# Queries turned by VectorE and regrouped through DRAM, causal chunks of 32 queries, weighted sums directly ahead of scores

## What is computed

```
q = (x @ wq.T)  32 heads of 32;   k, v = x @ wk.T, x @ wv.T   8 heads of 32
q = q * cos + rotate_half(q) * sin          (k the same)
scores = q k^T / sqrt(32), causal;  attn = softmax(scores);  out = attn v
x = layernorm(x + out @ wo.T)
```

## Time and profile before

| | |
|---|---|
| median of 3 runs | 1434.85 us (1432.27 to 1437.24) |
| the profiled execution | 1439.9 us |
| its span, first to last instruction | 1438.1 us |
| busy share PE / DVE / ACT / POOL | 95% / 76% / 65% / 69% |
| DMA | 213.03 MB, mean 148 GB/s |
| last matmul of part 1 ends | about 784 us into the span |

### The profile page before, as it was taken

The page is one execution under the profiler, slowest core; times in us unless marked ns, Lnnn a source line. Parts: engine busy times, 40 slices in busy tenths (PEclk is TensorE's granted clock), DMA queues, the critical chain, the costliest instruction groups (busy, mean ns, idle before and its releaser), DMA issues. The chain is left out here.

```text
span 1438.1 us, 32297 instructions
## 1 busy us (share of the span) xinstructions
PE 1370.1 (95%) x8288; PEld 1061.4 (74%) x8288; DVE 1092.5 (76%) x3869; ACT 932.5 (65%) x3258; POOL 985.9 (69%) x936
## 2 busy tenths in 40 slices
PE   6899999999999999999985899999999999999995
PEld 4677777777777777777753688888888888888874
DVE  5677777777777777777766477878887788887784
ACT  5678878788787887878765354555554455555542
POOL 3677767777677776777754566777766777776753
PEclk9999999999999999999996899999999999999997
DMA  6345445454454544545465857656666766666751
GB/s 227 113 121 156 122 139 152 119 155 122 141 152 119 152 125 141 151 119 153 125 179 164 218 145 170 165 153 163 159 159 165 175 150 159 165 156 162 157 117 44
DMA packets 108861, 213.03 MB, mean 148 GB/s; under 512 B 26640, under 2 KB 32272, under 8 KB 108816
## 3 DMA queue, kind: packets, MB, share of 16 engines
q1 hardware_dynamic: 108816, 212.51, 54.0%
HBM read 131.83 MB, written 34.47 MB: 116 GB/s over the span
## 5 line engine op out<-in xcount | busy, mean ns | idle before, releaser
L432 PE MATMUL wo_ps<-weights,halves 128*128 128x512 f32 x2304 | 573.8, 400 | 11.9 <-DVE weights L611 11.8
L432 PEld LDWEIGHTS wo_ps<-weights,halves 128*128 128x128 f32 x2304 | 423.8, 189 | 129.3 <-issue 34.3
L694 ACT ACTIVATE pexp<-sm,smin 128x128 f32<-128x128 f32 x1024 | 398.7, 393 | 119.1 <-DVE smin L562 118.4
L1039 PE MATMUL wo_ps<-weights,halves 128*128 128x512 f32 x1488 | 401.1, 402 | 2.0 <-DVE yz L1142 2.0
L811 POOL TENSOR_TENSOR pn<-pexp,prec 128x512 f32<-128x512 f32 x256 | 267.8, 1046 | 151.6 <-DVE prec L569 151.5
L1392 POOL TENSOR_TENSOR prods<-prod,prods 128x512 fp32r<-128x512 f32 x192 | 259.9, 1362 | 134.0 <-ACT prods L1286 129.1
L1039 PEld LDWEIGHTS wo_ps<-weights,halves 128*128 128x128 f32 x1488 | 273.4, 190 | 61.2 <-issue 3.7
L562 DVE CUSTOM_DVE_ANT_0 sm<-s_ps,mask_t 128x128 f32<-128x128 f32 x1024 | 231.8, 281 | 80.0 <-PE s_ps L462 80.0
L1286 ACT CAST prods<-prod 128x512 fp32r<-128x512 f32 x192 | 118.8, 621 | 165.9 <-DVE prod L1176 129.4
L1176 DVE TENSOR_TENSOR prod<-att,x 128x512 f32<-128x512 f32 x192 | 186.2, 985 | 14.0 <-DMA att<-sim_scratch 11.1
L694 ACT ACTIVATION_READ_ACCUMULATOR pexp<-sm,smin 128x1 f32 x1024 | 194.8, 190 | 0.0
(11 more groups left out here) (99 smaller groups left out, 1668.6 us busy)
## 6 DMA issues: line engine op xcount, KB each, us to landing
att<-sim_scratch SPq DMA_DIRECT2D x192, 252.0 KB
pt<-blocks SPq DMA_DIRECT2D x640, 64.0 KB, 2.0
ctx_t<-in_ctx SPq DMA_DIRECT2D x32, 576.0 KB, 4.5
raw<-in_xT SPq DMA_DIRECT2D x32, 512.0 KB, 3.7
raw<-ot_scratch SPq DMA_DIRECT2D x32, 512.0 KB, 6.6
xn<-in_x SPq DMA_DIRECT2D x32, 512.0 KB, 7.2
out<-late SPq DMA_DIRECT2D x32, 512.0 KB, 6.2
ot_scratch<-ot SPq DMA_DIRECT2D x63, 256.0 KB, 2.1
```

What stands on the lines that cost most here:

```text
L432: mm = pe.matmul(qkv_ps[(par + g) % 2][:], xs[:, par, xl, k], w_sb[:, wl, g, k], start=(k == 0 and n == 0), stop=(k == KT - 1 and n == 2))
L694: ins = nc.scalar.activation(pexp[:, c % 2, i * P:(i + 1) * P], sm[:, c % 2, i * P:(i + 1) * P], ACT.Exp, bias=smin[:, c % 2, i:i + 1], sc ...
L1039: mm = pe.matmul(wo_ps[n][:], os_t[:, par, ol, k], wo_sb[:, wl, k, n * BANK:(n + 1) * BANK], start=(k == 0 and m == 0), stop=(k == KT - 1 ...
```

## The change

Queries are no longer turned by PE and copied by ACT. DVE transposes them in blocks of 32x32 (`turn_q`, now DVE's), SP writes the blocks to DRAM (`send_q`) and fetches them back in four DMAs, regrouped so that a partition holds one dimension of a head (`fetch_q`). A chunk is now a block of 32 queries, for four query heads of each of four key heads, in the order of 128, 96, 64 and 32 keys (`TB`, `chunk`), so masks, exponentials, scaling and turning are as wide as the keys that these queries see. The probabilities too go by way of DRAM: two stores for a half (`send_p`), four fetches (`fetch_p`). On PE `weigh` stands directly ahead of `score` in one burst in slots 8 and 20 (11 and 23 in step 1, 5 and 17 in step 32). The keys' rotation is written into the free half of `rot1`. `square` and `neighbour` of the first two batches are put later, inputs `x` are loaded one step earlier, and `load_ctx(2)` and the sums' store of batch 1 stand at the end of SP's step 1. In diff form, the parts spoken of below (waits of the first step and of the last ones are left out):

```diff
+TB = (3, 2, 1, 0)
+    p_dram = nc.dram_tensor("p_scratch", [2, NU, P, QB, QB, NI, SB], F32, kind="Internal").ap()
+    q_dram = nc.dram_tensor("q_scratch", [2, NU, P, NI, NJ, SB], F32, kind="Internal").ap()
...
+    qb = (sb("qb0", [P, BANK])[:], xn0[:, BANK:D])
-    blocks = sb("blocks", [P, NU, QB, NJ, NI, SB])
-    pt = sb("pt", [P, NU, QB, NJ, NI, SB])
+    blocks = sb("blocks", [P, NU, QB, QB, NI, SB])
+    pt = sb("pt", [P, NU, NJ, QB, NI, SB])
...
+    SCORE_AT, FIRST_SCORE_AT, LAST_SCORE_AT = 8, 11, 5
+    def chunk(c):
+        u, j = divmod(c, NC // NU)
+        return u, TB[j], (TB[j] + 1) * SB
...
 @block.sync
-        def move_p(a, u):
-            wait(sp, turned, after(a, NC, NJ * (u + 1)))
-            wait(sp, pv_done, after(a - 1, NU, u + 1))
-            for qb in range(QB):
-                for kb in range(qb + 1):
-                    sp.dma_start(pt[kb * SB:(kb + 1) * SB, u, qb], blocks[qb * SB:(qb + 1) * SB, u, kb]
+        def send_q(t, par, u):
+            wait(sp, q_turned, after(t, NU, u + 1))
+            sp.dma_start(q_dram[par, u], qb[u].rearrange("p (i j q) -> p i j q", i=NI, j=NJ)).then_inc(q_out[u], 16)
+        def fetch_q(t, par, u):
+            wait(sp, scored, after(t - 1, NU, u + 1))
+            wait(sp, q_out[u], after(t, 16, 16))
+            for i in range(NI):
+                dst = qt[i * DH:(i + 1) * DH, u].rearrange("p (b n) -> p b n", b=QB)
+                src = q_dram[par, u, :, i].rearrange("(b d) j q -> d b (j q)", b=QB)
+                sp.dma_start(dst, src).then_inc(qt_in[u], 16)
+        def send_p(a, par, u, part):
+            keys, rows = ((slice(0, QB), slice(2, QB)), (slice(0, 2), slice(0, 2)))[part]
+            wait(sp, turned, after(a, NC, NJ * u + 2 * part + 2))
+            sp.dma_start(p_dram[par, u, :, keys, rows], blocks[:, u, keys, rows]).then_inc(p_out[u], 16)
+        def fetch_p(a, par, u):
+            wait(sp, pv_done, after(a - 1, NU, u + 1))
+            wait(sp, p_out[u], after(a, SENT, SENT))
+            for kb in range(QB):
+                src = p_dram[par, u, :, kb, kb:].rearrange("(j k) b i q -> k j b i q", j=NJ)
+                sp.dma_start(pt[kb * SB:(kb + 1) * SB, u, :, kb:], src).then_inc(p_in[u], 16)
...
 @block.tensor, step(t, par)
-                    if s % (NJ * PERIOD) == 1:
-                        score(a, 1 - par, s // (NJ * PERIOD))
-                    if s == 9:
-                        turn_q(a, 1)
-                    if s == 9:
-                        weigh(b, par, 0)
-                    if s == 17:
-                        weigh(b, par, 1)
-                    if s == 17:
-                        turn_k(t)
-                    if s == 22:
-                        turn_q(t, 0)
+                if valid(b):
+                    if s % (NJ * PERIOD) == burst:
+                        weigh(b, par, s // (NJ * PERIOD))
+                if valid(a):
+                    if s % (NJ * PERIOD) == burst:
+                        score(a, 1 - par, s // (NJ * PERIOD))
+                    if s == 20:
+                        turn_k(t, par)
...
 @block.vector
+        def turn_q(t, u):
+            wait(dve, roped, after(t, NG, 2 + u))
+            wait(dve, q_out[u], after(t, 16, 0))
+            dve.transpose(qb[u].rearrange("p (i j q) -> p i j q", i=NI, j=NJ), qn[u].rearrange("p (j i d) -> p i j d", j=NJ, i=NI)).then_inc(q_turned, 1)
...
                 if p == 0 and valid(a):
                     rotate(a, 1 - par, 2)
                 if p == 0 and valid(b):
                     invert(b, NC - 1)
-                if p == 5 and valid(t):
+                    turn_p(b, NC - 2)
+                    turn_p(b, NC - 1)
+                if p == 0 and valid(a):
+                    turn_q(a, 1)
+                if p == 0 and valid(t):
+                    rotate(t, par, 0)
+                if p == NJ and valid(a):
+                    invert(a, NJ - 1)
+                if p == NJ and valid(t):
                     rotate(t, par, 1)
+                if p == NJ and valid(a):
+                    turn_p(a, NJ - 2)
+                    turn_p(a, NJ - 1)
+                if p == NJ and valid(t):
+                    turn_q(t, 0)
                 if valid(a):
                     mask_min(a, p)
-                if p > 0 and valid(a):
+                if p % NJ > 0 and valid(a):
                     invert(a, p - 1)
...
-                if p < BEHIND and valid(b):
-                    turn_p(b, NC - BEHIND + p)
-                if p >= BEHIND and valid(a):
+                if p % NJ >= BEHIND and valid(a):
                     turn_p(a, p - BEHIND)
-                if p == 2 and valid(t):
-                    rotate(t, par, 0)
...
 @block.scalar
-        def copy_q(t, u):
-            wait(act, q_turned, after(t, NU, u + 1))
-            wait(act, scored, after(t - 1, NU, u + 1))
-            nc.scalar.copy(qt[:, u], turn_ps[:]).then_inc(qt_in, 1)
...
-                if p == 3 and valid(b):
+                if p == 1 and valid(b):
                     read_ot(b, 0)
-                if p == 6 and valid(b):
+                if p == 5 and valid(b):
                     read_ot(b, 1)
...
 @block.gpsimd
-                if p == 5 and valid(t):
-                    add_q(t, par, 0)
                 if p > 0 and valid(a):
                     scale(a, p - 1)
+                if p == 4 and valid(t):
+                    add_q(t, par, 0)
```

More of the change, by code:

```diff
@@ L206, in part1 @@
     q_turned = sem("q_turned")
-    qt_in = sem("qt_in")
+    q_out = [sem(f"q_out{u}") for u in range(NU)]
+    qt_in = [sem(f"qt_in{u}") for u in range(NU)]
     scored = sem("scored")
@@ L214, in part1 @@
     turned = sem("turned")
+    p_out = [sem(f"p_out{u}") for u in range(NU)]
     p_in = [sem(f"p_in{u}") for u in range(NU)]
@@ L371, in step @@
             a, b = t - 1, t - 2
-            if valid(t + 1):
-                if not at_step(t, 0):
-                    load_x(t + 1, 1 - par)
+            first, second = at_step(t, 0), at_step(t, 1)
+            if first:
+                load_x(2, 0)
+                send_q(0, 0, 0)
+                fetch_q(0, 0, 0)
+                move_v(0, 0)
+            if valid(b):
+                send_p(b, par, 1, 1)
+            if valid(a):
+                send_q(a, 1 - par, 1)
+            if valid(t + 1) and not second:
                 load_ctx(t + 1)
@@ L393, in step @@
                 load_o(1)
[L394 removed]
+                wait(sp, q_out[1], 16 * B)
                 sp.dma_start(xn0[:], x[0]).then_inc(xn_in[0], 16)
[L396 to L402 removed]
             if at_step(t, B - 1):
                 load_later(2)
+            if valid(t + 2) and not first:
+                load_x(t + 2, par)
             if valid(a):
[L406 removed]
+                send_p(a, 1 - par, 0, 0)
+            if valid(t) and not first and not second:
+                send_sums(t)
+            if valid(a):
+                send_p(a, 1 - par, 0, 1)
             if at_step(t, B - 1):
@@ L410, in step @@
                 load_later(9)
+            if at_step(t, B - 1):
+                load_later(4)
+            if valid(t) and not first:
+                send_q(t, par, 0)
+            if valid(a):
+                fetch_p(a, 1 - par, 0)
+            if valid(t) and not first:
+                fetch_q(t, par, 0)
             if valid(b) and not at_step(b, B - 1):
@@ L413, in step @@
                 sp.dma_start(ot_dram[b, :, BANK:D], ot[:, 1]).then_inc(ot_out[1], 16)
-            if at_step(t, B - 1):
-                load_later(4)
+            if valid(t) and not first:
+                move_v(t, par)
+            if second:
+                load_ctx(2)
+                send_sums(1)
+            if valid(a):
+                send_p(a, 1 - par, 1, 0)
         steps(sp, step, 0, LAST, LEAD, TAIL)
@@ L539, in rotate @@
             wait(dve, roped, after(t, NG, g - 1))
+            if g == 2:
+                wait(dve, k_turned, after(t, 1, 1))
             q3 = src[:, 0:width].rearrange("p (h d) -> p h d", d=DH)
@@ L1470 @@
         "rope": rope_tables(),
-        "mask": np.where(keys[None, :] > keys[:, None], np.float32(MASKED), np.float32(0.0)),
+        "mask": np.where(keys[None, :] > places[:, None], np.float32(MASKED), np.float32(0.0)),
         "ident": np.eye(P, dtype=np.float32),
```

118 lines of the change are left out of this document (56 added, 62 removed).

## The result

The change makes the kernel slower: 1490.7 us (median of 4 runs, 1489.1 to 1493.46), against 1434.73 before in the same comparison; the ratio is 1.0388, 95% interval [1.0373, 1.0403]. The forecast was 1478 us with a range of 1440 to 1512. The profiled execution took 1491.97 us with a span of 1489.0.

The account below looks back on a forecast made before the run. The prediction took DVE's list, with ACT and POOL inside it, as the new bound: steps +38, start +10.1, last steps -4, sum +44 on 1439.9 us, 1484, or 1478 us in median terms; range 1440 to 1512.

Parts of the forecast that it names:

- PE's own step of 21.0: Part 1, PE: a step falls from 22.50 to 21.0 us without query transposes, with fewer projection stretches and narrower scores.
- The narrower scores: Part 1, PE: the scores of a half, 1.11 us before, get 0.15 us shorter with fewer keys streamed.
- The loop of 23.85: Part 1, steps 2 to 30: DVE's list, with ACT and POOL inside it, takes 23.85 us a step for 22.50; +38.
- Where PE idles: Part 1: PE idles 2 to 3 us in each step, released at the group that waits for DVE's rotation.
- rival B: Part 1: trips through DRAM become the bound, landing later; step 24.95 us, +31, 1509 us; chance 0.14.
- The trips: Part 1: stores and fetches through DRAM stay hidden with 1.9 and 2.1 us to spare; nothing added.
- Rival C: Part 1: pauses drop PE's clock to 1.2 GHz, costing about 4 us a step, some 1510 us; chance 0.04.
- The start: First steps of part 1: first queries by DRAM +1.4, late context +7.3, the step's own +1.35; +10.1 us.
- The wait for the context: Start of part 1: POOL waits for `load_ctx(2)`, now last in SP's step 1; +7.3 us.
- The tail: Last two steps of part 1: narrower chunks and six issues for ten, against two extra landings; -4 us.
- The conversion: Whole kernel: 1484 us for the profiled execution, which lay 5.05 above the median, becomes 1478 us in median terms.

Follow-up runs that it names:

- the reordered kernel: The changed kernel with all its operations and transfers kept but the lists of DVE, ACT, POOL and SP reordered: 1429.8 us, ratio 0.9964.
- Two passes for three: The changed kernel with one of three matmuls of every projection left out: 1491.03 us, ratio to before 1.0386.

## Why the prediction was right, and where it was not

- *PE's own step of 21.0.* Right: the reordered kernel's first steps take 20.99 and 20.99. The narrower scores gave a little less than taken: a half takes 1.02 (424.86 to 425.88), 0.09 less than before, for 0.15.
- *The loop of 23.85.* Right, 23.87 in the step shown and 23.89 on average; moving ACT's and POOL's work out of it by order alone took 0.96 off the step, where 1.1 was expected. Waits where forecast: DVE on ACT ahead of reciprocals (mostly 1.0 to 1.15), on POOL ahead of the turned queries (0.93) and of the last turned chunk of a step (1.50), none on scores. Not seen: that the branch through ACT and POOL was 0.4 us behind the one summed.
- *Where PE idles.* Wrong in place. The sign named was a group waiting for DVE's rotation; in the steady steps PE waits 0.8 to 2.5 us at the weighted sums, and the trace names the landing of `pt`. Read alone, such a row looks like rival B. Two passes for three made this wait longer (40.1 us for 20.7 from 300 to 500) and the kernel no slower: it was slack of PE, not the bound.
- *The trips.* Hidden, as forecast, with a DMA share of 0.83 from 100 to 700 us for 0.81 (the sum took 0.47 where the earlier trace rows reads 0.48). The terms were off both ways: issue 0.43 for 0.62, and landing of a fetch 3.8 to 4.7 for 2.0. The Trainium skill's page "DMA: Bandwidth & Descriptors", section "Latency and other measured facts", has 2 us for access to memory at high load. The trace agrees in part: the fetches landed 1.8 to 2.7 us later than the 2.0 taken from the earlier trace rows, but they are of another kind than the moves of that row, and the outputs' store, which both kernels have, landed only 1.4 later. That it did not decide is luck: two errors nearly cancel. So the slack came out at 2.4 and 2.2 us on average, for 1.9 and 2.1, with 0.3 to 1.0 where PE ran at the slow clock.
- *Rival C.* The slow clock came, after some pauses, and its price on PE shows (weighted sums 1.94 for 1.07, at a granted clock of 0.50). Its effect on the step does not: behind that very burst M4 to M0 is 11.66. It used up slack of PE.
- *The start*, +10.1: **over-sized**. Half of it came, +4.5. The wait for the context was 5.58 for 7.3, and of the 8.65 for it and the longer step 3.4 came. Why so little of the wait reached the time stays open.
- *The tail*, -4: **the step that failed**, by 12.8 us, and with the wrong sign. The forecast had weighed narrower chunks and fewer issues against two landings; it had not gone through SP's list in step 31, where a load that waits for a buffer stands ahead of the queries' store, nor through PE's in step 32. Both orders stand in the code. Moving both gave back about 7 of 8.8 us in the trace.
- *The conversion.* The sum was 1484 on the profiled execution's scale, where 1491.97 was measured, 8 us more: -5.6 at the start, +12.8 in the tail, +0.9 in the rest. The other 4.6 of the 12.7 us between 1478 and 1490.7 are no mechanism: before's profiled execution lay 5.05 over its median, after's only 1.27, and the remainder is rounding. The start and the tail partly cancel, so the total looks better than its parts; the steps do not need that luck.

## What to carry to other kernels

When an engine's list is rearranged so that one group of work ends before the next begins, sum the dependency chain across that border on all engines, not only the busy time; here every engine got less to do and the kernel 3.9% slower. The same transfers and operations in another order, with a second buffer for the sums, made it 1.4% faster than before. Follow each branch into the operation that closes the loop, since removing one only gains up to the next, and go through the in-order queues of the first and last steps by themselves: there one blocked entry held everything behind it, and two such blocks hid one another in the measured time until both were gone.
